# First attention of a two-layer model on one core: softmax sums by matmul, division after the value product, tiled matmuls, and four head maxima applied as an activation bias

## What is computed

```python
# x = x + L0_xattn(layernorm(x), ctx_768, ...)         16 heads of 16 channels, 77 keys
q  = (x @ Wq.T + bq).reshape(b, l, 16, 16)
kv = (y @ Wkv + bkv).reshape(b, 77, 16, 32);  k, v = kv[..., :16], kv[..., 16:]
att = softmax(einsum('blhd,bmhd->blmh', q, k) / sqrt(16), axis=2)
out = einsum('blmh,bmhd->blhd', att, v).reshape(b, l, 256)
return out @ Wo.T + bo
```

## Time and profile before

| | |
|---|---|
| median of 3 runs | 885.13 us (884.46 to 886.65) |
| the profiled execution | 889.84 us, of which 887.7 us are the span from the first to the last instruction |
| stage A's units | first maximum at 25.9 us, all engines through the barrier at about 171 us |
| TensorE busy in 25.9 to 171.2 us | 119.5 of 145.3 us |
| VectorE busy there | 117.0 of 145.3 us |
| ScalarE, GpSimd busy there | 55.4 and 58.7 us |
| granted TensorE clock there | 0.99 of full, one piece at about half |

### The profile page before, as it was taken

The page is one execution under the profiler, slowest core; times in us unless marked ns, Lnnn a source line. Parts: engine busy times, 40 slices in busy tenths (PEclk is TensorE's granted clock), DMA queues, the critical chain, the costliest instruction groups (busy, mean ns, idle before and its releaser), DMA issues.

```text
span 887.7 us, 10616 instructions
## 1 busy us (share of the span) xinstructions
PE 724.3 (82%) x3332; PEld 417.2 (47%) x3332; DVE 584.6 (66%) x1732; ACT 294.8 (33%) x641; POOL 355.8 (40%) x372
## 2 busy tenths in 40 slices
PE   4689877864798998989979866868798899999972
PEld 3456544562344444444547623323253374647651
DVE  3888887435756373462657788999795497664265
ACT  2354333210372451815412253555420212021210
POOL 2344434103588685685410246787700021112020
PEclk9999999955898997988979977998889799999996
DMA  8910000210122221121288100020010000000002
GB/s 219 400 31 1 1 12 3 80 62 24 53 72 72 69 81 49 65 81 58 78 256 317 44 2 0 1 95 1 0 48 0 1 1 0 1 0 1 0 1 95
DMA packets 33086, 52.77 MB, mean 59 GB/s; under 512 B 8718, under 2 KB 21582, under 8 KB 32776
## 3 DMA queue, kind: packets, MB, share of 16 engines
q1 hardware_dynamic: 28040, 36.76, 12.6%
q0 software_dynamic: 4992, 15.34, 5.1%
HBM read 36.62 MB, written 15.47 MB: 59 GB/s over the span
## 4 chain that ended last, share of the span: by engine, by line
PE 54%; DVE 25%; POOL 6%; issue 6%; ACT 5%; DMA 2%; POOLq 1%; SPq 0%; DVEq 0%; ACTq 0%
PE ps L459 50%; DVE arena L1883 4%; DVE arena L1880 3%; ACT arena L934 2%; DVE arena L1496 2%; DVE arena L1492 2%; DVE arena L329 2%; DMA arena<-scr_z,idsU 2%; DVE kp L1385 1%; DVE arena L1385 1%; DVE arena L1391 1%; POOL arena L1274 1%; POOL scr_g L1266 1%; PE ps L514 1%; DVE X L1391 1%
## 5 line engine op out<-in xcount | busy, mean ns | idle before, releaser
L459 PE MATMUL ps<-arena 64*32 64x32 f32 (+6 forms) x2296 | 543.6, 396 | 29.9 <-DVE arena L1609 8.7
L459 PEld LDWEIGHTS ps<-arena 128*128 128x128 f32 (+3 forms) x2296 | 267.3, 164 | 231.5 <-issue 182.7
L934 ACT ACTIVATE arena<-ps 128x256 f32<-128x256 f32 (+6 forms) x255 | 120.5, 487 | 280.5 <-PE ps L459 136.0
L324 POOL TENSOR_SCALAR rstd<-mv 128x4 f32<-128x4 f32 (+2 forms) x34 | 14.6, 430 | 236.8 <-DVE mv L318 183.4
L1736 DVE TENSOR_TENSOR arena<-ps,arena 128x512 f32<-128x512 f32 x39 | 27.0, 691 | 103.3 <-ACT arena L1048 91.1
L1232 POOL TENSOR_TENSOR arena<-arena 128x616 f32<-128x616 f32 x32 | 40.2, 1256 | 80.0 <-DVE arena L1504 80.0
L1266 POOL DMA_INDIRECT scr_g<-arena,destU x39 | 50.1, 1285 | 37.7 <-DVE arena L1736 30.4
L1259 POOL DMA_INDIRECT arena<-scr_z,idsU x39 | 45.9, 1177 | 40.8 <-PE ps L652 28.7
L1883 DVE MATCH_REPLACE8 arena<-arena 128x77 f32<-128x77 f32 x256 | 54.1, 222 | 0.0
L1048 ACT ACTIVATE arena<-ps 128x512 f32<-128x512 f32 x39 | 23.3, 597 | 92.2 <-PE ps L459 92.0
L988 ACT ACTIVATE arena<-arena 128x616 f32<-128x616 f32 x32 | 23.0, 717 | 75.7 <-DVE arena L1496 75.7
(11 more groups left out here) (196 smaller groups left out, 988.9 us busy)
## 6 DMA issues: line engine op xcount, KB each, us to landing
arena<-in_w1t SPq DMA_DIRECT2D x8, 1024.0 KB, 14.0
arena<-scr_g SPq DMA_DIRECT2D x8, 1024.0 KB, 7.9
X<-in_x SPq DMA_DIRECT2D x2, 1024.0 KB, 5.9
scr_z<-arena SPq DMA_DIRECT2D x4, 512.0 KB, 3.3
arena<-in_c_dftf SPq DMA_DIRECT2D x1, 2048.0 KB, 14.9
arena<-in_L_xattn_W SPq DMA_DIRECT2D x2, 1024.0 KB, 6.3
out<-X SPq DMA_DIRECT2D x16, 128.0 KB, 1.8
scr_k<-arena SPq DMA_DIRECT2D x4, 256.0 KB, 8.2
```

Of the source, the lines that this page charges most:

```text
L459: return pe.matmul(o, l, r, start=first, stop=final)
L934: return a.activation(o, i, ACT.Copy)
```

## The change

The softmax is no longer normalised before the value product. The probabilities stay unnormalised, a second set of matmuls (`sums`) gives each head's sum in the same layout as the values' output, and VectorE divides once for each group of 4 units (`divide`): a reciprocal of 128x512 from PSUM and a multiply of 128x512. That takes away, for each unit, VectorE's sum and reciprocal and GpSimd's 616-column multiply. VectorE subtracts the maximum for 4 heads only (308 columns); for the other 4 GpSimd negates and scales the maxima (a 128x4 instruction), and ScalarE runs one exponential of 77 columns for each head, straight from PSUM, with that as its bias. The two score matmuls contract 64 rows each (the two halves of the array), and `values` and `sums` are each 8 matmuls that write 32 output partitions (4 strips, two chunks each) where `values` had 5 that wrote 128. `project` uses banks 6 and 7. A mask `sk` for the sums is built and transposed in the first block, `Pb` has 3 buffers for 4, and the order of work between the units is written anew.

```diff
-        Pb = ra.take(4, GW)
+        Pb, sk = ra.take(PBUF, GW), ra.take(NCH, P)
...
                 if u >= 2:
                     pe.wait_ge(s["scores_read"], u - 1)
+                    pe.wait_ge(s["probs_exp"], u - 1)
...
                 for c in range(2):
-                    ins = mm(ps[:, 2 * (u % 2) + c, 0:BW], qT[:, j % 2, g, t * P:(t + 1) * P],
-                             kblk[:, g, j // 2, c * BW:(c + 1) * BW], True, True)
+                    half = slice(c * P // 2, (c + 1) * P // 2)
+                    ins = mm(ps[:, 2 * (u % 2) + c, 0:BW], qT[half, j % 2, g, t * P:(t + 1) * P],
+                             kblk[half, g, j // 2, c * BW:(c + 1) * BW], True, True)
...
-            def values(j, g, chunks):
-                for c in chunks:
...
-                    ins = mm(bank(6), vk[0:m, j // 2, g, c, :], PT[0:m, g, c, :], c == 0, c == NCH - 1)
+            def values(j, g):
+                pe.wait_ge(s["pt_sb"], turned_all(8 * j + 4 * g + 3))
+                for r in range(2):
+                    for q in range(4):
+                        m, cols = vkeys(q + r), slice(32 * q, 32 * q + 32)
+                        ins = mm(ps[cols, 6, :], vk[0:m, j // 2, g, q + r, cols], PT[0:m, g, q + r, :], r == 0, r == 1)
+                ins.then_inc(s["oT_ps"], 1)
+            def sums(g):
+                for r in range(2):
+                    for q in range(4):
+                        m, cols = vkeys(q + r), slice(32 * q, 32 * q + 32)
+                        ins = mm(ps[cols, 7, :], sk[0:m, q + r, cols], PT[0:m, g, q + r, :], r == 0, r == 1)
+                ins.then_inc(s["oT_ps"], 1)
...
+                if st == 0:
+                    if j:
+                        pe.wait_ge(s["oT_sb"], 2 * j - 1)
+                    queries(j, 1, 7)
+                elif st == 1 and ahead:
+                    pe.wait_ge(s["qT_sb"], 2 * j + 2)
+                    turn_z(j + 1, 0, 7)
+                    if j:
+                        turn_z(j + 1, 1, 6)
+                elif st == 2:
...
-                    a.wait_ge(s["scores_read"], S + 1)
-                    a.activation(Pb[:, S % 4, :], Pb[:, S % 4, :], ACT.Exp, scale=1.0 / math.sqrt(DH0))
+                    a.wait_ge(s["max_neg"], S + 1)
+                    for h in range(HG // 2):
+                        a.activation(Pb[:, S % PBUF, BW + h * S2:BW + (h + 1) * S2], ps[:, 2 * (S % 2) + 1, h * S2:(h + 1) * S2],
+                                     ACT.Exp, bias=nmA[:, S % PBUF, h:h + 1], scale=1.0 / math.sqrt(DH0))
+                    a.wait_ge(s["scores_read"], S + 1)
+                    a.activation(Pb[:, S % PBUF, 0:BW], Pb[:, S % PBUF, 0:BW], ACT.Exp, scale=1.0 / math.sqrt(DH0))
...
+            p.wait_ge(s["rows_in"], 16 * 9)
+            for t in range(8):
+                bias_A(t)
             for u in range(NU):
-                p.tensor_tensor(pv, pv, smA[:, u % 4, :].unsqueeze(2).broadcast_to([P, HG, S2]), ALU.mult)
+                p.tensor_scalar(nmA[:, u % PBUF, :], mxA[:, u % PBUF, HG // 2:HG], -1.0 / math.sqrt(DH0), None, ALU.mult)
...
+            def divide(j, g):
+                v.wait_ge(s["oT_ps"], 2 * (2 * j + g) + 2)
+                if j:
+                    v.wait_ge(s["oA_ps"], 2 * j)
+                own.done(v.reciprocal(OT[:, g, :], bank(7)))
+                own.settle()
+                v.tensor_tensor(OT[:, g, :], bank(6), OT[:, g, :], ALU.mult).then_inc(s["oT_sb"], 1)
...
+                if j and st == 3:
+                    divide(j - 1, 1)
+                elif j and st in (4, 5):
+                    add_A(j - 1, st - 4)
...
+                elif st == 7:
+                    divide(j, 0)
```

More of the change, by code:

```diff
@@ L50 @@
 ARENA = 37144
+PBUF = 3
 SCAT = 4
@@ L555, in _ @@
             queries(0, 0, 7)
-            queries(0, 1, 6)
-            pe.wait_ge(s["qT_sb"], 2)
-            for S in range(NU + 3):
+            for S in range(NU + 2):
                 j, st = S // 8, S % 8
@@ new lines, in _ @@
+                if S == NU:
+                    break
+                if st == 0:
+                    if j:
+                        pe.wait_ge(s["oT_sb"], 2 * j - 1)
+                    else:
+                        pe.wait_ge(s["qT_sb"], 1)
+                    queries(j, 1, 7)
[4 more added lines that the diff above has]
+                        turn_z(j + 1, 1, 6)
+                elif st == 2:
+                    if j == 0:
+                        pe.wait_ge(s["zTA_sb"], 3)
+                        turn_z(1, 1, 7)
+                    elif ahead:
+                        queries(j + 1, 0, 7)
+                    if j:
+                        values(j - 1, 1)
+                elif st == 3:
+                    if j == 0:
+                        queries(1, 0, 7)
+                    else:
+                        pe.wait_ge(s["qT_sb"], 2 * j + (3 if ahead else 2))
+                        sums(1)
+                elif st == 4:
+                    if j:
+                        project(j - 1, 0)
+                    else:
+                        pe.wait_ge(s["kblk_ready"], 9)
+                        pe.wait_ge(s["qT_sb"], 3)
+                        turn_s(0)
+                elif st == 5:
+                    if j:
+                        project(j - 1, 1)
+                    else:
+                        pe.wait_ge(s["vk_sb"], 6)
+                        turn_s(1)
@@ L591, in _ @@
                 elif st == 6:
                     if j:
[L593 to L596 removed]
+                        pe.wait_ge(s["xA_done"], 2 * j - 1)
+                    else:
+                        pe.wait_ge(s["vk_sb"], 7)
+                    values(j, 0)
                 elif st == 7:
                     if j:
[L599 to L601 removed]
@@ L602, in _ @@
-                    values(j, 0, (0,))
-            values(NBLK - 1, 1, range(NCH))
-            pe.wait_ge(s["xA_done"], 2 * NBLK - 2)
+                        pe.wait_ge(s["xA_done"], 2 * j)
+                    sums(0)
+            turn_P(NU - 1)
+            pe.wait_ge(s["oT_sb"], 2 * NBLK - 1)
+            values(NBLK - 1, 1)
+            sums(1)
             project(NBLK - 1, 0)
@@ L1007, in _ @@
-            put_o(NBLK - 1, 1)
+                if S < NU:
+                    a.wait_ge(s["max_neg"], S + 1)
[3 more added lines that the diff above has]
+                    a.wait_ge(s["scores_read"], S + 1)
+                    a.activation(Pb[:, S % PBUF, 0:BW], Pb[:, S % PBUF, 0:BW], ACT.Exp, scale=1.0 / math.sqrt(DH0))\
+                        .then_inc(s["probs_exp"], 1)
+                    if st == 0:
+                        put_q(j, 1, 7)
+                    if st == 1 and ahead:
+                        put_z(j + 1, 0, 7)
+                        if j:
+                            put_z(j + 1, 1, 6)
+                    if st == 2 and ahead:
+                        if j:
+                            put_q(j + 1, 0, 7)
+                        else:
+                            put_z(1, 1, 7)
+                    if S == 3:
+                        put_q(1, 0, 7)
+                    if S in (4, 5):
+                        put_s(S - 4)
```

201 lines of the change are left out of this document (80 added, 121 removed).

## The result

The change makes the kernel slower: 896.79 us (four executions, 891.3 to 898.05) against 884.8 us before in the same session, a ratio of 1.0121 [1.0092, 1.015]. The forecast was 880 us, faster.

A forecast was written before the change was run, and what follows sets the result against it. No single bound: VectorE and TensorE alternate, and the new order couples them at each division. Middle -1.0, start +0.1, end -5.5 give -6.4 us; with one clock fall -5: 884.8 profiled, 880 us median, range 870 to 900.

The forecast's parts named there:

- Division, 4.05 us from the line of the earlier trace: VectorE's divide: reciprocal of 512 columns 3.35 us at 6.25 ns a column, multiply 0.69; eight divisions 32.4 us.
- idle time of TensorE that it counted: TensorE waiting for the divided output behind `sums`: about 2.9 us idle in each division.
- Strips and halves overlap in full: TensorE's tiles run side by side: scores 0.52 us a unit instead of 1.03, `values` and `sums` 1.72 us a call.
- Rivals 1 and 3: Strips overlap only in pairs: +27 us, about 907, chance 0.10; score halves do not overlap: +15, 895, chance 0.07.
- Clock: "I count one": TensorE's granted clock in stage A falls once for all the division idles, a fall costing up to 1.7 us.
- Rival 2: TensorE's clock falls in most divisions: five to eight falls, +7 to +12 us, 886 to 892; chance 0.17.
- Half-blocks of 15.1 and 17.6 us, 32.7 a block: Stage A's middle, division to division: 11.1 and 4.05 us, then 13.6 and 4.05, in series.
- 1.3 us added for `split_bias`: `split_bias` after unit 21 falls into a division's way for 1.3 us; after 17 and 25 it has room.
- The half-block of block 3, 13.3 in the walk: Last half-block between divisions in stage A, where no next block follows: 13.3 us instead of 17.6.
- Start 57.2 us: Start of stage A: first exponential at 30.3 us behind eight row biases, then ScalarE's pace; 57.2 where 57.1 before, no gain.
- End 12.3 us: End of stage A: division 4.05, two projections 3.44, addition and latency; 12.3 us where 17.8 before, gain 5.5.
- sum's -6.4: Whole program before any clock fall: middle -1.0, start +0.1, end -5.5, together -6.4 us.

The follow-up runs named there:

- untiled run: The change with five filling matmuls, late row biases and scores, values and sums over the whole array instead of tiles: 896.82 us, 1.037 of the kernel before.
- filled kernel: The change with five unread matmuls ahead of waits for a division and row biases moved later: 855.20 us (0.9898 of before); on another chip 878.78 us (0.9914).
- late biases: The change with GpSimd's first eight row biases moved behind units 1 to 4, 6 and 7, the next four behind 8 and 9: 890.81 us, 1.0031 of before.
- filled runs with the division in one piece: The change with five filling matmuls, division not cut: alone 0.9937 of before, with late row biases 0.9898 and 0.9914, with those and bias part undone 0.9901.
- second filled run with late biases: The change with five filling matmuls and late row biases, run again on another chip beside the loosened division: 878.78 us, 0.9914 of the kernel before.
- the one with the bias part undone: The change with filling and late row biases, but VectorE subtracting 616 columns and ScalarE taking one exponential of 616: 856.40 us, 0.9901 of before.
- other two filled runs: The change with five filling matmuls alone, 883.01 us (0.9937 of before), and its first run with late row biases too, 855.20 us (0.9898).

## Why the prediction was wrong

By its own steps:

- **Division, 4.05 us from the line of the earlier trace rows.** Right: 3.358 and 0.69. The idle time of TensorE that it counted was right too: 2.9 us counted, 2.79 measured at six of the eight.
- **Strips and halves overlap in full.** Right for the strips, nearly for the halves. Sixteen records of values, 0.43 us each if they came one after another, take 1.93 us with the tail. The second row shows the first four of them alone, the third the next four:

```profile
159.84 1.93 PE L461 MATMUL ps<-arena 128*32 128x512 f32 x16
159.84 0.64 PE L461 MATMUL ps<-arena 128*32 128x512 f32 x4
160.30 0.61 PE L461 MATMUL ps<-arena 128*32 128x512 f32 x4
```

  Four records start at once, on four strips, and the next four 0.46 us behind them. The untiled run prices all the tiles together at 10.5 us a block. Rivals 1 and 3 fall.

  The Trainium skill (TensorE: Matmul & The Clock Gate, The mechanism) has matmuls start and end strictly in order, and the same section says that tiles overlap. These rows don't contradict it: in the trace the sixteen records start and end in four groups of four, and no row shows a later matmul starting or ending ahead of an earlier one. What failed is the prediction's step from that rule to a call of twice 1.72 us, that the second record of a strip would hold up the next strip.
- **Clock: "I count one".** This is the step that failed. I took an idle of 2.60 us that had left the clock up, and one of some 4.2 us after which it fell, and put 2.9 on the side of the first, with one fall for all eight divisions. It fell in seven places, one of them twice as long: 12.2 us where the sum had 1.5. Rival 2 had the mechanism and its price for a fall (1.5 measured, up to 1.7 foreseen), and a chance of 0.17 that looks too low for an idle that comes eight times and lies between a harmless and a harmful one. The time, 896.79, lies above its 886 to 892, by about what the smaller terms below add.
- **Half-blocks of 15.1 and 17.6 us, 32.7 a block.** At full clock a block takes 33.97, so 1.3 too little. Scores and transposes take 1.41 us from start to start in a unit (84.12 to 84.84 is 0.72 for the scores, transposes 0.69), against 1.25 walked with the tile changes: 1.3 us in eight units. Not all of that is the change of tile. The second pair of score records starts 0.36 us behind the first, where 308 columns took 0.256 before, with no change of tile between them:

```profile
84.12 0.53 PE L461 MATMUL ps<-arena 64*128 64x308 f32 x2
84.48 0.43 PE L461 MATMUL ps<-arena 64*128 64x308 f32 x2
```

  This was read from spacings, and not tested by itself. The 1.3 us added for `split_bias` didn't show: block 2, which has it, takes 33.97 us in the filled kernel, like block 1. The half-block of block 3, 13.3 in the walk, takes 14.7 between its reciprocals there.
- **Start 57.2 us.** 59.19. The mechanism was right (the first exponential at 31.33 instead of 30.3, behind the biases), and the late biases showed that it costs some 3.5 to 5 us; the walk after it was 1 us short, and had no clock falls in it (6.8 us of block 0 were at half).
- **End 12.3 us.** 16.5 in the change, 12.45 with full clock: right but for the clock.

Without clock falls the stage would end at 59.19 + 111.05 = 170.2 us, 0.9 us before the old one, where the walk had 164.7. So the sum's -6.4 was really about -1 (start 2.0, blocks 3.4, end 0.1 us missing), and the clock adds 12.2: 182.4. The small terms took the gain, and the clock made it a clear loss.

## What to carry to other kernels

An instruction that moves from every unit to every fourth unit is not only a sum of durations: if the engine before waits for it and the one behind too, all of it lies on the path, and a wait that repeats can take the clock down nearly each time. Look in such a case for what may run in the gap (even matmuls that nobody reads gave 1.8%), and attach each wait to the instruction that needs it: moving one wait from the reciprocal to the multiply behind it gave 1.1 and 2.1 us in blocks 1 and 2. Splitting the same work over tiles gave 10.5 us a block in the changed kernel and nothing in stage A of the kernel before: ask first whether the others wait for TensorE.

## What the runs showed of the hardware

- A reciprocal on VectorE costs by the column at the same rate from 16 to 512 columns: 16 take 0.253 us, 128 take 0.953, 256 take 1.76, 512 take 3.36; a plain copy of 512 takes 0.69.
- Matmuls on four strips of 32 columns, and on two halves of 64 rows, run side by side in fp32, although each is two records: sixteen records of 512 columns in 1.93 us, four of 308 columns in 0.79 us where 128 rows took 1.20.
- TensorE idle for 2.79 us between stretches of dense work, six times in the change, was followed by half clock for 3.4 us five times and left the clock up once. With one filling matmul in the gap, eight pieces of 3.4 us became four; behind the waits with five, in blocks 1 to 3 of the filled runs with the division in one piece, no fall was seen. The unfilled idle of 1.99 us came with a fall in the change, in the second filled run with late biases and in the one with the bias part undone, and with none in the other two filled runs.
- Going from Exp to Ln and back on ScalarE put a table load of 1.28 us ahead of each, 3.8 us for the two functions on 512 columns.
- Four exponentials of 77 columns from PSUM with a bias take 0.97 us at a mean of 339 ns each, so about 0.21 from start to start.
